# Fused attention and mixture-of-experts kernel: three sets of steps placed elsewhere inside each row's order

## The reference

```
h = layernorm(x)
q = rope(rms_norm(h @ wq)); k = rope(rms_norm(h @ wk)); v = h @ wv          # 16 query heads, 4 key heads, 128 wide
k_ctx = rms_norm(ctx @ wk_ctx);  v_ctx = ctx @ wv_ctx                        # 128 context tokens per row
scores = q @ [k_ctx, k] / sqrt(128) + causal mask on the second half
x = x + (softmax(scores) @ [v_ctx, v]) @ wo
x = x + moe(layernorm(x))                                                    # 8 experts, top 2, and a shared expert
```

## Time and profile before

| | |
|---|---|
| median of 3 runs | 361.87 us (360.94 to 363.26) |
| profiled execution, its own time | 360.24 us |
| its span in the trace | 357.6 us |
| granted PE clock, mean | 0.991 |
| busy: PE / DVE / ACT / POOL | 91% / 88% / 74% / 47% |
| period of a row in the loop | 35.5 us |

### The profile page before, as it was taken

One profiled execution on the slowest core, in us unless ns is written; L12 is line 12 of the kernel. 1 busy time (PEld: TensorE's weight loads), 2 busy tenths in 40 slices (PEclk: granted clock), 3 DMA queues, 4 the chain that ended last, 5 costly groups with the idle time before them and its releaser, 6 DMA issues.

```text
span 357.6 us, 7425 instructions
## 1 busy us (share of the span) xinstructions
PE 326.2 (91%) x2292; PEld 222.8 (62%) x2296; DVE 313.5 (88%) x602; ACT 263.6 (74%) x917; POOL 166.4 (47%) x241
## 2 busy tenths in 40 slices
PE   6677698799999999999999999999999999999994
PEld 5354465377657765766576667666766687856452
DVE  1779999998999899989998999899989997875763
ACT  4668989575987598759875987698769866747541
POOL 4367656653655365536542644274417331063530
PEclk9999989999999999999999999999999999999998
DMA  6977000000024002400300000000000000046783
GB/s 185 385 242 235 18 0 2 1 2 15 1 61 115 15 0 68 107 15 3 59 0 15 0 0 0 15 0 0 0 0 0 1 2 0 2 88 90 135 165 114
DMA packets 34834, 19.24 MB, mean 54 GB/s; under 512 B 24056, under 2 KB 32256, under 8 KB 34816
## 3 DMA queue, kind: packets, MB, share of 16 engines
q1 hardware_dynamic: 34816, 19.02, 20.8%
HBM read 12.20 MB, written 1.05 MB: 37 GB/s over the span
## 4 chain that ended last, share of the span: by engine, by line
PE 37%; DVE 22%; ACT 19%; issue 11%; POOL 6%; DMA 2%; SPq 1%; DVEq 1%; ACTq 0%; POOLq 0%
PE proj L1362 10%; ACT probs L548 8%; PE pt_ps L1325 6%; DVE probs L982 6%; PE turn L1271 4%; POOL q_rot L774 3%; PE o_ps L1335 3%; DVE nmax L970 3%; DVE pT_lo L908 3%; PE proj L1182 3%; ACT pT_hi L459 3%; PE sc_ps L1292 3%; ACT kc_junk L492 2%; DVE q_t L899 2%; DMA wq<-in_L_xattn_wq_dram 2%
## 5 line engine op out<-in xcount | busy, mean ns | idle before, releaser
L548 ACT ACTIVATE probs<-sc_ps,nbias,q_r 128x256 f32<-128x256 f32 x128 | 70.8, 573 | 2.8 <-DVE nbias L974 2.8
L774 POOL TENSOR_TENSOR q_rot<-q_t 128x512 f32<-128x512 f32 x32 | 42.4, 1325 | 41.3 <-DVE q_t L901 40.5
L982 DVE TENSOR_SCALAR probs<-probs,rden 128x256 f32<-128x256 f32 x128 | 51.0, 459 | 1.1
L459 ACT ACTIVATE pT_hi<-pt_ps 128x512 f16<-128x512 f32 x64 | 34.8, 597 | 10.2 <-PE pt_ps L1325 10.2
L492 ACT ACTIVATE q_junk<-proj 128x128 bf16<-128x128 f32 x128 | 34.1, 298 | 10.8 <-DVE q_t L901 10.8
L908 DVE SCALAR_TENSOR_TENSOR pT_lo<-pt_ps,pT_hi 128x512 f16<-128x512 f32 x64 | 41.0, 681 | 0.1
L1182 PE MATMUL proj<-wq_hi,xT 128*128 128x512 f16 x128 | 38.2, 380 | 2.7 <-DVE wq_lo L892 2.2
L970 DVE TENSOR_REDUCE nmax<-sc_ps 128x4 f32<-128x1024 f32 x32 | 38.8, 1214 | 1.5 <-PE sc_ps L1314 1.5
L459 ACT ACTIVATE qT_hi<-turn 128x512 f16<-128x512 f32 x32 | 19.5, 609 | 21.6 <-PE turn L1271 21.6
L731 POOL TENSOR_TENSOR q_r<-q_me,power 128x4 f32<-128x4 f32 x32 | 33.4, 1044 | 2.5
L1325 PE MATMUL pt_ps<-ident,probs 128*128 128x128 f32 x256 | 34.2, 278 | 0.2
(11 more groups left out here) (222 smaller groups left out, 870.9 us busy)
## 6 DMA issues: line engine op xcount, KB each, us to landing
wq<-in_L_xattn_wq_dram SPq DMA_DIRECT2D x4, 512.0 KB, 7.9
w<-in_L_ffn_w_dram SPq DMA_DIRECT2D x2, 1024.0 KB, 9.9
wq<-in_L_xattn_wo_dram SPq DMA_DIRECT2D x1, 2048.0 KB, 8.2
ctx_b<-in_ctx_dram SPq DMA_DIRECT2D x8, 128.0 KB, 2.0
out_dram<-x_all SPq DMA_DIRECT2D x4, 256.0 KB, 2.2
x_all<-in_x_dram SPq DMA_DIRECT2D x1, 896.0 KB, 11.3
wkc<-in_L_xattn_wk_ctx_dram SPq DMA_DIRECT2D x1, 512.0 KB, 4.0
wk<-in_L_xattn_wk_dram SPq DMA_DIRECT2D x1, 512.0 KB, 5.0
```

Source lines behind the costliest of these rows:

```text
L459: return nc.scalar.activation(out_, in_, ACT.Copy, scale=scale)
L548: last = nc.scalar.activation(probs[:, h, :], sc_ps[:, h, :], ACT.Exp, bias=nbias[:, h:h + 1], scale=q_r[:, g, h:h + 1], accum_out=den[:, ...
L774: nc.gpsimd.tensor_tensor(q_rot[:], q_t1[:], q_t2[:], ALU.add).then_inc(q_added, 1)
L982: last = nc.vector.tensor_scalar(probs[:, h, :], probs[:, h, :], rden[:, h:h + 1], None, ALU.mult)
```

## The change

Only the order of steps changes; no step is added or taken away.

- In g = 0, PE makes `v` directly after `vc`, ahead of the mix of the row before's last unit. ACT makes `vc_copy` and `v_copy` directly after the exponentials, ahead of `q_squares`. DVE makes `v_low` ahead of `normalise`, and `vc_low` ahead of `o_low`.
- In g = 2, ACT makes `kc_squares` between the two pairs of exponentials, and `kc_scale` and `k_squares` ahead of `o_copy`. DVE makes `k_turn` ahead of `normalise`. The `o_low` of this group moves to g = 3, behind `q_low`.

```diff
 (ACT)
-                    exps(b, g, (kc_copy, k_copy) if g == 3 and not last else ())
+                    exps(b, g, () if last else ((), (), (kc_squares,), (kc_copy, k_copy))[g])
                     if g == 1 and not first and not last:
                         ln_high(b + 1)
-                    if g == 2 and not last:
-                        kc_squares(b + 1)
+                    if g == 0:
+                        vc_copy(b)
+                        v_copy(b)
                     if ahead_of(b, g, 2, last):
                         q_squares(*ahead_of(b, g, 2, last))
...
-                    if g == 0:
-                        v_copy(b)
-                    if (g or not first) and not (g == 3 and last):
-                        o_copy(u - 1, (g - 1) % G)
                     if g == 2 and not last:
                         kc_scale(b + 1)
                         k_squares(b + 1)
+                    if (g or not first) and not (g == 3 and last):
+                        o_copy(u - 1, (g - 1) % G)
...
-                    if g == 0:
-                        vc_copy(b)
 (DVE)
+                    if g == 3:
+                        o_low(u - 2, G - 3)
...
+                    if g == 0:
+                        v_low(b)
...
+                    if g == 2 and not last:
+                        k_turn(b + 1)
                     normalise(b, g)
...
-                    if g == 2 and not last:
-                        k_turn(b + 1)
...
                     if g == 0:
-                        v_low(b)
-                    if g or not first:
+                        vc_low(b)
+                    if g != 2 and (g or not first):
                         o_low(u - 1, (g - 1) % G)
...
-                    if g == 0:
-                        vc_low(b)
 (PE)
                         vc(b)
+                        if first:
+                            pe.wait_ge(w_lo, G + 2)
+                        v(b)
                         if not first:
                             mix(u - 1, G - 1)
-                        else:
-                            pe.wait_ge(w_lo, G + 2)
-                        v(b)
```

## The result

The changed kernel is slower: its median is 375.46 us (375.11 to 378.71, 7 runs) against 362.43 us for the kernel before in the same comparison (360.74 to 363.68, 7 runs). The ratio of the comparison is 1.0395, 95% interval 1.0363 to 1.0427, which on 361.87 us is +14.3 us (+13.1 to +15.5). The two medians by themselves are 13.0 us apart, a ratio of 1.036, just under that interval; so the loss is known as about 13 to 15.5 us and no better. The forecast was 373.0 in a range of 367 to 377.

The account below looks back on a forecast made before the run. Waits between PE and DVE, each near 90% busy, bound it. 2.35 + 0.70 + 5 x (0.85 + 0.70) + 0.85 = 11.65 us on 360.24 gives 371.9, scaled to the median 373.6, taken as 373; range 367 to 377.

Parts of the forecast that it names:

- The mix holds the value copies: g = 0: ACT's copies into v_hi wait until the mix ends at 143.30; DVE waits 2.0 us for v_hi.
- +0.85 per row: g = 0: PE's turn_probs starts at 146.5 instead of 145.69; the maximum of g = 2 slips by the same.
- The division gets short again: g = 0: POOL's q_rot pass ends well ahead, so the division takes 1.14 us instead of 1.70.
- DVE idle 2.0 us: g = 0: DVE, done with ln_st at 142.5, waits 2.0 us for v_hi in front of v_lo.
- g = 2 and g = 3, +0.70: Wait for k, division under q_rot and moved o_low put the next row's maximum +0.70 us behind that of g = 2.
- First product 1.4: g = 2: the division's first product waits for the end of POOL's q_rot pass and lasts about 1.4 us.
- the division escapes q_rot: Rival, g = 2: pass and products miss each other, 0.35 per row stays instead of 0.70, 371 us; chance 0.15.
- Row 0, +2.35: Row 0: division behind v_lo delays the scaled input xs, +2.0; g = 2 and g = 3 cost +0.35.
- Row 1, +0.70: Row 1: g = 0 costs 0, since v fills PE's pause; 0.70 comes in g = 2.
- row 7, +0.85: Row 7: it has g = 0's part only, +0.85 us.
- The clock rival: PE's new waits in g = 0 make its clock fall in every row: 9 us more, 382; chance 0.04.
- Rivals that forecast a gain in g = 0: Mix no hindrance, 0.57 us gained per row: 357.8, or near 361.9 with g = 2's loss; chance 0.05 each.

Follow-up runs that it names:

- the kernel with the mix first: The changed kernel with only PE's old order put back in g = 0 (mix ahead of v): 372.95 us, ratio 1.0335.
- the squares alone: The kernel before with kc_squares between the exponentials in g = 2 as the only change: 373.4 us, one run.
- rotation-only: The kernel before with k_turn ahead of the division in g = 2 as the only change: 365.94 us, one run.
- low-piece-only: The kernel before with o_low of g = 2 moved into g = 3 as the only change: 366.32 us, one run.
- the control: The kernel before with v_hi and v_lo doubled for even and odd rows, its own order kept: 361.72 us, ratio 1.0014.

## Why the prediction was right, and where it was short

The sign, the mechanism in g = 0 and the first wait in g = 2 held, and the median of 375.46 lies in the range; the profiled execution, 378.71, lies above it. The forecast of a ratio of 1.032 (11.65 of 360.24) was low; measured is 1.0395, interval from 1.0363 (1.036 by the medians).

**The mix holds the value copies: right.** v_hi starts with the mix's end, ACT is the releaser of DVE's wait, and taking the buffer conflict away gives back 1.62 us per row. **Its size, +0.85 per row: too small,** 1.25 measured in row 3 (and 1.01 with g = 0 alone). Set against the row's first maximum, my chain and the trace part as follows:

| step | forecast | after | the step's own error |
|---|---|---|---|
| mix ends | 5.71 | 5.88 | +0.17 |
| vc_hi starts | 5.76 | 5.98 | +0.05 |
| v_lo starts | 6.86 | 7.17 | +0.09 |
| first product | 7.66 | 7.98 | +0.01 |
| products end | 8.81 | 9.12 | -0.01 |
| turn_probs starts | 8.86 | 9.26 | +0.09 |

I had let the row start 0.05 us later against its maximum; it is 0.16 (with the g = 0 edits alone it is nothing, as before). That is 0.11 of the first line's 0.17. The other errors are handovers. From the end on one engine to the start on a waiting one takes 0.10 us (PE to ACT), 0.10 (ACT to DVE) and 0.14 (DVE to PE) in the rows of after; I had counted 0.05 to none. Three new waits in one chain make three new handovers. At turn_probs the slip is 1.21 us (9.26 against 8.05 before); another 0.04 comes by the maximum of g = 2.

**The division gets short again: right,** 1.14 us. **DVE idle 2.0 us:** 2.41, by the same 0.31 by which v_lo starts late in the table, and because ln_st ended 0.1 earlier than forecast.

**g = 2 and g = 3, +0.70: right in size,** 0.73 (0.71 with the g = 2 edits alone). DVE idle 0.5 before the rotation: 0.45. First product 1.4: 1.32. Key sum 0.68: 0.68. Cutting the pass shows that the collision stretches the division, but not that it is the whole price: 0.28 of the 0.73 go with it and 0.45 stay. The rival "the division escapes q_rot" had this right, 0.35 less and ACT the later one. The main text had it wrong where it says that o_copy behind the key squares costs nothing because ACT's next copies wait for PE: it read the copy at 166.6, and the queries' copy at 165.79 ahead of it did not wait. The 0.49 us that it names for the other case is close to the 0.45. That this copy is all of the 0.45 is not shown, as no kernel has the pass cut and o_copy put back.

**Row 0, +2.35: +4.07.** Its g = 0 term of 2.0 was right where the clock held (2.09 in the kernel with the mix first), and g = 2 with g = 3 gave +0.30 here and +0.67 with the g = 2 edits alone (0.35 forecast). The other 1.7 us go with the clock's fall in g = 0: the mix-first kernel has the same code in row 0 and no fall. I had set 1.5 to 4 as the bounds for row 0 with "shift the clock's fall" as a reason; 4.07 is just above them. The fall in g = 2 that went away gave nothing back: with the g = 0 edits alone there was no fall in g = 2 either, and that group took 10.22 us, against 10.21 in the kernel before with the fall.

**Row 1, +0.70: +0.98; row 7, +0.85: +1.20.** Row 1's g = 0 was counted at nothing; with g = 0 alone it costs 0.28. Row 7's is the same undersized g = 0 term.

**The clock rival** (a fall in every row, 382): did not happen. PE's waits of 0.59 and 0.62 us in the rows left the clock at 1.00.

**Added up:** from 11.65 to 18.4 in the two profiled executions are 2.0 in rows 2 to 6, 0.3 in row 1, 0.4 in row 7, 1.7 for the clock in row 0, and 2.35 ahead of the first maximum, in code that the change does not touch; that part took 26.3 to 29.7 us over all the traces here. Without these last two the profiled difference is 14.3 us, against 13.0 (medians) to 14.3 (ratio) measured over seven runs. That the two figures of 14.3 are equal is no proof. Only one of the seven has a trace, but the mean granted clock is on record for all: 0.983 there, 0.990 to 0.993 in the other six. By my estimate from these means and the spans (twice the missing share of the span) that is 13 us at half clock in the profiled execution and 5 to 8 us in the others, so none of them had all of its falls; which they lacked stays open. The range held, since its ends came from the terms' bounds; 9 to 15 covered 14.3 near its upper end, while the central 11.65 was too low in the g = 0 terms of rows 1 to 7.

**Rivals that forecast a gain in g = 0** fell by what the prediction held against them, the mix's end. The gain that they named is real (0.59 per row), but only with a second buffer, which is not in this change.

## What to carry to other kernels

Before moving a producer ahead, look for the last reader of the buffer that it overwrites: if a consumer of the old contents stands beside it in the same group, the move only turns cover into waiting, and doubling the buffer (here 0.59 us per row gained instead of 1.01 to 1.25 lost) decides the sign. Price a chain with new waits with one handover for each engine change, 0.10 to 0.14 us in these rows. In g = 2, a collision that was taken off one instruction fell in every reordering on the next one beneath the same pass; in g = 0 nothing that collides was left beneath it, and the division got short. So a move out of a collision gains only in the second case. And when a cost is removed, read the same removal in the kernel before: what stays between the two is the cost of the next in line.

## What the runs showed of the hardware that was not expected

- A string of four DVE products of 0.34 us beside one POOL pass of 1.27 us: in every trace in which the pass began within the string or up to 0.1 us ahead of it, one product lasted 1.32 to 1.46 us, the first, the second or the third of them according to the pass's start. Where the pass began 0.28 to 0.50 us ahead, the first product lasted 1.14 to 0.91 us. A product that started up to 0.05 us before the pass still stood for it (1.46 us in row 1 with the squares alone); one that started 0.07 us before it did not. A pass that came 0.07 or 0.41 us behind the string's start was itself only 0.14 or 0.06 us longer.
- The granted clock fell or held in g = 0 of row 0 behind the same 1.96 us pause of PE. It fell there in after, with g = 0 alone and with two buffers (that group 12.29 us each), and also in the rotation-only and low-piece-only kernels, whose code of that group is the one before (10.10 us); it held in the kernel before, with the g = 2 edits alone, in the control, in the two-buffer kernel that keeps row 0's order and with the squares alone (8.51 to 8.52 us), and with the mix first (10.61 us). What decides it stays open; it is worth 1.6 to 1.7 us of one execution. A fall in g = 0 of row 1, in three of the traces, goes with 11.4 us in the control and with the squares alone and 12.3 us with the low piece alone, against 10.49 us for the same code without it in the kernel before. The fall in g = 2 of row 0 cost nothing that can be measured (10.21 against 10.22 us).
